# Graph network kernel on one core: the first two relation pairs projected node group by node group, and two passes over the nodes moved to GpSimd

## The reference, cut to what matters

```python
h = relu(layernorm(x)); agg = segment_sum(gate * core, dst)
x = x + layernorm(agg + h) * gamma + beta          # end of the first layer
h = relu(layernorm(x))                             # input of the second
proj = einsum('ni,rio->rno', h, Wf)                # 16 relations, 3125 nodes each
m = (proj[etype, src] + bias) / degree[dst]        # gathered by edge
x = x + 2 * (h @ loop_weight) + self_bias + segment_sum(m, dst) + backward pass
```

## Time and profile before

| What | us |
|---|---|
| median of three executions | 3847.81 |
| the lowest and the highest of them | 3843.88, 3848.78 |
| the profiled execution | 3849.95 |
| its span in the trace | 3848.1 |
| PE busy in the span | 3288.7 |
| DVE busy in the span | 2579.7 |
| POOL busy in the span | 2340.2 |
| ACT busy in the span | 976.2 |

### The profile page before, as it was taken

One profiled execution on the slowest core, in us unless ns is written; L12 is line 12 of the kernel. 1 busy time (PEld: TensorE's weight loads), 2 busy tenths in 40 slices (PEclk: granted clock), 3 DMA queues, 4 the chain that ended last, 5 costly groups with the idle time before them and its releaser, 6 DMA issues.

```text
span 3848.1 us, 74572 instructions
## 1 busy us (share of the span) xinstructions
PE 3288.7 (85%) x21136; PEld 2831.0 (74%) x21137; DVE 2579.7 (67%) x3930; ACT 976.2 (25%) x1654; POOL 2340.2 (61%) x2362
## 2 busy tenths in 40 slices
PE   6999999999999996998777778878857778787776
PEld 4999999999999995887665566666645666665654
DVE  6888888888888887887766673333354444444444
ACT  3555555555555544442000000000010000000000
POOL 1666655666665660002776677777777777777775
PEclk8999999999999998999989899999989999999999
DMA  5666666666565652664555557555533333333333
GB/s 173 174 171 171 172 171 168 171 168 169 167 169 164 170 160 84 208 209 160 158 163 153 151 154 164 166 157 161 160 97 105 104 102 98 100 105 104 104 105 114
DMA packets 322741, 569.88 MB, mean 148 GB/s; under 512 B 73895, under 2 KB 218389, under 8 KB 322581
## 3 DMA queue, kind: packets, MB, share of 16 engines
q0 software_dynamic: 137984, 411.19, 38.5%
q1 hardware_dynamic: 182732, 154.33, 12.2%
q10 hardware_dynamic: 1864, 2.52, 0.2%
HBM read 452.43 MB, written 115.41 MB: 148 GB/s over the span
## 4 chain that ended last, share of the span: by engine, by line
PE 64%; DVE 15%; issue 10%; POOL 4%; DMA 3%; DVEq 2%; ACT 1%; SPq 1%; ACTq 0%; POOLq 0%
PE pc L671 14%; PE pa L680 13%; PE pa L719 7%; PE pu L657 5%; DVE tops L1210 5%; PE pu L719 4%; PE pg L643 4%; DVE key L1213 4%; PE pg L719 4%; POOL fa L422 4%; PE pu L651 3%; PE pc L666 2%; DMA fa<-proj,gslot 2%; PE pu L775 2%; PE pg L775 1%
## 5 line engine op out<-in xcount | busy, mean ns | idle before, releaser
L422 POOL DMA_INDIRECT fa<-proj,gslot x1568 | 1503.5, 959 | 882.0 <-issue 436.8
L405 POOL DMA_INDIRECT fa<-ptab,slot x784 | 832.9, 1062 | 576.5 <-issue 298.9
L680 PE MATMUL pa<-fa,onehot 128*128 128x258 f32 x1760 | 471.0, 416 | 212.3 <-DVE onehot L994 141.4
L671 PEld LDWEIGHTS pc<-ws,hr 128*128 128x128 f32 x4704 | 607.1, 188 | 16.8
L671 PE MATMUL pc<-ws,hr 128*128 128x256 f32 x4704 | 614.0, 279 | 0.0
L994 DVE SCALAR_TENSOR_TENSOR fa<-pc,base,src_f 128x512 f32<-128x512 f32 x406 | 303.6, 751 | 450.0 <-PE pa L719 320.0
L680 PEld LDWEIGHTS pa<-fa,onehot 128*128 128x128 f32 x1760 | 349.6, 205 | 319.2 <-issue 264.0
L719 PE MATMUL pa<-fa 128*128 128x258 f32 x1568 | 373.5, 380 | 0.0
L719 PEld LDWEIGHTS pa<-fa 128*128 128x128 f32 x1568 | 297.0, 189 | 45.2
L719 PE MATMUL pu<-fa 128*128 128x258 f32 x784 | 198.9, 397 | 120.7 <-DVE acc L1051 82.5
L1000 DVE TENSOR_TENSOR fa<-fa,pc 128x1024 f32<-128x1024 f32 x196 | 239.4, 1221 | 92.4 <-PE pc L671 92.3
(11 more groups left out here) (151 smaller groups left out, 4934.9 us busy)
## 6 DMA issues: line engine op xcount, KB each, us to landing
proj<-fa SPq DMA_DIRECT2D x400, 256.0 KB, 2.3
fa<-in_ea_t SPq DMA_DIRECT2D x196, 128.0 KB
fa<-proj,gslot POOLq DMA_INDIRECT x1568, 2.8
fa<-ptab,slot POOLq DMA_INDIRECT x784
fa<-in_Wrel SPq DMA_DIRECT2D x32, 256.0 KB, 3.0
ptab<-fa SPq DMA_DIRECT2D x25, 256.0 KB, 2.0
out<-res SPq DMA_DIRECT2D x4, 768.0 KB
res<-in_x SPq DMA_DIRECT2D x1, 1792.0 KB, 20.4
```

The source lines that it names most:

```text
L405: pool.indirect_dma_start(pbuf[:, n % 2, j, :], None, ptab[:, :], bass.IndirectOffsetOnAxis(ap=slot[:, n, j:j + 1], axis=0)).then_inc(s_ga ...
L422: pool.indirect_dma_start(gbuf[:, n, j, 0:H], None, proj[k - 1][:, :], bass.IndirectOffsetOnAxis(ap=gslot[:, at, j:j + 1], axis=0)).then_i ...
L671: last = nc.tensor.matmul(pc[:, j, :], uT[:, par, a, j // 2, kk, j % 2 * P:(j % 2 + 1) * P], w2s[:, c, kk, :], start=False, stop=(j == jj ...
L680: last = nc.tensor.matmul(pa[:, bank, 0:width], keys[:, at, j, :], rows[:, j, :], start=(n == 0), stop=(n == len(todo) - 1))
```

## The change

Pairs 0 and 1 are both projected group by group. PE does the 5 blocks of a group for pair 0, three transposes of the next group, and then the 5 blocks for pair 1 with the other two transposes behind the first two of them. Within a slot the uses alternate between the pairs (`slot_use`, `projected`). ACT's `node_group` gets two loops: the first normalises the blocks of a group and copies out pair 1 of two groups before, alternating; the second copies out pair 0 and the transposed blocks. The low weights of pair 1 move up to DVE's third node group, and those of pair 2 from the head of the sort to behind its third step. The memset and the self bias addition move from DVE to GpSimd, behind the last transposed block; DVE waits for them just ahead of `add_own`. SP loads the weights of pairs 2 and 3 ahead of the first stores. The core of the diff:

```diff
+        def slot_use(q, b):
+            return 2 * (b // GB) + q if piped(q) else 5 * q + b // 5
+        def projected(q, b):
+            return 2 * GB * (b // GB) + GB * q + b % GB if piped(q) else NB * q + b
...
-            with sp.Fori(0, NQ // 4) as i:
+            for q in range(2):
+                sp.wait_ge(s_wlo, q + 1)
+                load_weights(q + 2, q)
+            for g in range(NB // GB):
+                for q in range(2):
+                    store_projections(q, 0, group(g))
+            with sp.Fori(1, NQ // 4) as i:
                 relations(i, 0)
...
+            pool.wait_ge(s_hT[1], NB)
+            nc.gpsimd.memset(acc[:, :, :], 0.0).then_inc(s_zero[0], 1)
+            nc.gpsimd.tensor_tensor(res[:, :, :], res[:, :, :], sbias_b[:, :].unsqueeze(1).to_broadcast([P, NB, H]),
+                                    ALU.add).then_inc(s_sb, 1)
             pool.wait_ge(s_zero[0], 1)
...
                 if past(q, 2):
-                    act.wait_ge(s_proj, NB * (q - 1))
+                    act.wait_ge(s_proj, 2 * NB - GB if isinstance(q, int) and q == 2 else NB * (q - 1))
...
                 if g == 0:
                     weights_high(0, 0, 0)
+                    weights_high(1, 1, 0)
+                for n in range(GB):
+                    if 1 <= g <= NB // GB:
                         normalise(2, group(g - 1)[n], res, ACT.Relu)
+                    if g >= 3:
+                        evacuate(act, nc.scalar.copy, 1, group(g - 3)[n])
+                for n in range(GB):
+                    if 2 <= g <= NB // GB + 1:
+                        evacuate(act, nc.scalar.copy, 0, group(g - 2)[n])
+                    if 1 <= g <= NB // GB:
+                        transposed_high(group(g - 1)[n])
...
             weights_high(2, 0, 1)
-            for b in range(NB):
-                evacuate(act, nc.scalar.copy, 1, b)
+            node_group(NB // GB + 2)
...
+            for b in group(0):
+                transposes(1, b)
             for g in range(NB // GB):
...
                 for b in group(g):
                     pe.wait_ge(s_hT[1], b + 1)
                     project(0, 0, b, 0)
+                later = group(g + 1) if g + 1 < NB // GB else []
+                for b in later[:3]:
+                    transposes(1, b)
+                if g == 0:
+                    pe.wait_ge(s_wlo, 2)
+                for n, b in enumerate(group(g)):
+                    project(1, 1, b, 0)
+                    for t in later[3 + n:4 + n]:
+                        transposes(1, t)
...
-                if g == 1:
-                    weights_low(0, 0)
+                if g in (1, 2):
+                    weights_low(g - 1, g - 1)
...
-            weights_low(1, 1)
...
-            nc.vector.memset(acc[:, :, :], 0.0).then_inc(s_zero[0], 1)
-            nc.vector.tensor_tensor(res[:, :, :], res[:, :, :], sbias_b[:, :].unsqueeze(1).to_broadcast([P, NB, H]),
-                                    ALU.add).then_inc(s_sb, 1)
...
+                    if also and n == 2:
+                        weights_low(2, 0)
...
-            weights_low(2, 0)
-            for q in range(2):
-                sort_relation(q)
+            sort_relation(0, also=True)
+            sort_relation(1)
...
+            dve.wait_ge(s_zero[0], 1)
+            dve.wait_ge(s_sb, 1)
             for b in range(NB):
                 add_own(b)
```

More of the change, by code:

```diff
@@ L251, in turned, with piped @@
             return bank.rearrange("p (k n) -> p k n", k=HK)
-        def evacuate(eng, copy, q, b):
[L255 to L260, removed]
+        def piped(q):
+            return isinstance(q, int) and q < 2
+        def slot_use(q, b):
+            return 2 * (b // GB) + q if piped(q) else 5 * q + b // 5
+        def projected(q, b):
+            return 2 * GB * (b // GB) + GB * q + b % GB if piped(q) else NB * q + b
+        def evacuate(eng, copy, q, b):
+            n, use = b % 5, slot_use(q, b)
+            eng.wait_ge(s_proj, projected(q, b) + 1)
+            if past(use, 1):
+                eng.wait_ge(s_pst[n], 16 * use)
             copy(pstage[n].rearrange("p r f -> p (r f)"), pslots[n]).then_inc(s_pev[n], 1)
@@ L324, in load_weights, with store_projections @@
                                  wv[bass.ds(q, 1), :, kk, :, :].rearrange("q p r f -> (q p) r f")).then_inc(s_wrel[par], 16)
-            def store_projections(q, d):
-                for b in range(NB):
+            def store_projections(q, d, blocks=range(NB)):
+                for b in blocks:
                     n = b % 5
-                    sp.wait_ge(s_pev[n], 5 * q + b // 5 + 1)
+                    sp.wait_ge(s_pev[n], slot_use(q, b) + 1)
                     sp.dma_start(pv[d][bass.ds(q - d * (NQ // 2), 1), :, b, :, :].rearrange("q p r f -> (q p) r f"),
@@ L549, in node_group @@
                     weights_high(0, 0, 0)
-                for n in range(GB + 1):
-                    if 1 <= g <= NB // GB and n < GB:
+                    weights_high(1, 1, 0)
+                for n in range(GB):
+                    if 1 <= g <= NB // GB:
                         normalise(2, group(g - 1)[n], res, ACT.Relu)
[L553 to L556, removed]
+                    if g >= 3:
[5 more added lines that the diff above has]
+                        transposed_high(group(g - 1)[n])
                 if g < NB // GB:
                     sqrt_var(2, g, GB * g, GB * (g + 1))
-                elif g == NB // GB:
-                    weights_high(1, 1, 0)
             for g in range(NB // GB + 2):
@@ L765, in project @@
             def project(q, u, b, d):
-                n = b % 5
-                if b >= 5 or past(q, 1):
-                    pe.wait_ge(s_pev[n], 5 * q + b // 5)
+                n, use = b % 5, slot_use(q, b)
+                if past(use, 1):
+                    pe.wait_ge(s_pev[n], use)
                 if d:
@@ L783, in forward_relations @@
                         project(2 * i + u, u, b, 0)
+            for b in group(0):
+                transposes(1, b)
             for g in range(NB // GB):
-                for b in group(g):
-                    transposes(1, b)
                 if g == 0:
@@ L792, in _ @@
                     project(0, 0, b, 0)
-            pe.wait_ge(s_wlo, 2)
-            for b in range(NB):
-                project(1, 1, b, 0)
+                later = group(g + 1) if g + 1 < NB // GB else []
[7 more added lines that the diff above has]
+                        transposes(1, t)
             with pe.Fori(1, NQ // 4) as i:
@@ L1219, in keep_sorted, with sort_relation @@
                 nc.vector.tensor_copy(srt[:, bass.ds(8 * it, 8 * n)], tops[:, 0:8 * n]).then_inc(s_sort, 1)
-            def sort_relation(q):
+            def sort_relation(q, also=False):
                 before = (2 * S1 + 1) * q
```

2 lines of the change are left out of this document (removed).

## The result

The changed kernel took 3856.74 us (median of 17 runs, 3850.31 to 3862.79), the kernel before 3844.61 in the same series (17 runs, 3840.15 to 3851.59). The ratio is 1.0030, with a 95% interval of 1.0022 to 1.0037: 12.1 us slower, 8.5 to 14.2. The forecast was 13.1 us slower, a median of 3860.9 in a range of 3849 to 3865. A second series, on another chip, gave 3856.57 beside 3847.01, ratio 1.0027 (1.0018 to 1.0037).

A forecast was written before the change was run, and what follows sets the result against it. The prediction took DVE's sort to end the stage, so its start and stops decide. Terms 2.9 + 0.4 + 1.7 + 8.1 = 13.1 us on 3847.81 gave 3860.9, range 3849 to 3865.

The forecast's parts named there:

- The rule: Whole stage: it ends when DVE's sort ends, 236 us after the sort starts; PE's gain does not count.
- the throttle of the last weight copy: End of the sort: the last weight copy ended only 2.1 us before DVE's subtraction that needs it.
- Steps 1 to 4: Node groups: PE stands 2.8 us ahead of groups 1 and 2; DVE's last transposed block comes 13.8 us later.
- Step 5: Behind three sort steps: DVE waits 4.1 us for pair 2's low weights; stage ends 2.9 us later.
- Step 6: Ahead of pair 3: PE idles about 12 us and may restart at its lower clock; 0 to 0.8, taken 0.4.
- Step 7: Node groups: PE's new gaps cause zero to two clock falls, 0 to 3.4 us; one taken, 1.7.
- Step 8: GpSimd: moved memset 4.9 us and addition 14.7 us, ending by 1559.3 to 1564.2, by itself free.
- Step 9: Pair 2's weight subtraction on DVE: held until GpSimd's addition ends; zero to 8.1 us, 8.1 taken.
- rival A: Pair 2's subtraction passes GpSimd's addition or is stretched only a microsecond: 5.0 us slower, 3852.8; chance 0.34.
- steps 1 to 7: Node groups to pair 3: sort delay 2.9, PE lag 0.4 and clock fall 1.7, together 5.0 us.
- rival B: Node groups: PE has no gaps because normalisations come earlier; 5.2 us less, 3842.6; chance 0.08.
- Rivals B and C: B: node groups without PE gaps, 3842.6, 0.08. C: sort starts 13.6 us earlier, 3834; with other gains 0.05.

## Why the prediction was right, point by point

**The rule (the sort ends the stage): shown.** With the throttle of the last weight copy it foretold that 13.6 us less DVE work gives 2 and not 13.6 (1.6 measured) and that load added is seen in full (13.7 added, 14.2 measured). That PE's 12 us ahead of pair 3 cost nothing is read from the changed kernel's own trace: from 1561.56 to the sort's end DVE never stood longer than 0.5 us and never for a weight copy, and `own` still had to wait 5.75 us for DVE.

**Steps 1 to 4: right, slightly short.** Gaps of 2.54 and 2.57 against 2.8, released by ACT's slot copy. Group 1 started at 1500.22 (1499.7 laid out), group 2 at 1519.30 (1517.1 and one fall), group 3 at 1536.92 (1532.8 and one fall). The last transposed block came 18.1 later in the first trace and 16.3 to 16.7 in the two others, against 13.8 + 1.7 = 15.5.

**Step 5: right.** A wait of 4.33 against 4.1.

**Step 6: right.** 12.10 us of idle PE ahead of pair 3, and the lower clock behind it (4.99 against 2.88). It cost nothing, where 0.4 was put on it: no later subtraction waited for its weights.

**Step 7: right in kind, short in size.** Groups 1 and 2 both started slow in the first trace; I had taken one fall for 1.7. In the two later traces only group 1 starts slow (4.58 and 4.48), and group 2 fast (2.97 in both), behind the same gap of 2.55. Of the nine traces with this order five have the last transposed block at 86.5 and four at 85.0. So the term was 1.7 or 3.4.

**Step 8: half right.** The memset took 5.50 (4.9 from the rows), the addition 14.33 (14.7). What failed is that the two follow one another: 6.92 us lie between.

**Step 9: wrong in this kernel.** Its 8.1 us were the largest term of the sum. The exclusion is real (11.30 and 9.10 us when the addition comes first) but the subtraction started first and took 1.23 us, so the term measured nothing. So what happened is rival A's path, 5.0 forecast and 6 to 8 found in the stretch, while the medians moved by 12.1. The forecast of 13.1 came close because a term that did not occur made up for clock falls of which I took too few and for up to 4 us that I can't place. The sign and the place rest on steps 1 to 7. That the loss would be above 0.2% rested on step 9 (0.46 of the 0.52), and this, like the closeness of the number, was luck. The step's other reason, that gathers of 1062 and 959 ns show GpSimd held by DVE, was not tested. In rival B, 45 blocks and 20 transposes from 1479.87 end at 1545.5 by the spacings given, not 1546.5; no chance hangs on that microsecond.

The Trainium skill, page "SBUF — State Buffer", section "Who interferes with whom", says that whichever of the two is second waits for the whole of the first. Three runs agree: the three held subtractions (11.30, 9.10 and 3.72 us) all ended 1.1 us after the addition. The page "GPSIMD Engine Reference" of the Trainium skill, section 2.1, speaks of about 6 us for the first call to a newly loaded kernel (there a routine of GpSimd's), with no instruction in the profile; the gaps here are 6.9 to 8.1 us, also marked only "issue". Set into my lay-out, an estimate from that figure would not have settled the order: the addition would have started at 1544.6 + 4.9 + 6 = 1555.5, just ahead of the subtraction at 1556.1. It would have shown that the term hung on less than a microsecond.

**Rivals B and C** did not occur; no trace has the node groups free of gaps or the transposes at their old times.

## What to carry to other kernels

Find the queue that ends the stage, then ask what holds that queue back if it gets lighter: here 13.6 us of work removed gave 2, and 13.7 us added cost all of itself in the stretch. When work moves to another engine, list which instructions it will meet there; two short passes that each read two SBUF operands can cost the length of the longer one, depending on which starts first. And a queue order that helps one engine (PE's second pair between the transposes) has to be paid for on the engine that ends the stage, unless that engine's idle time is filled as well.

## What the runs showed of the hardware

The first addition on GpSimd started 6.9 to 7.6 us after the memset ahead of it had ended, in six traces. After a small addition earlier it started at once. In the three kernels where it waited for `s_wlo` at that point anyway (9.10, 7.34 and 8.05 us) it started 0.1 us after the subtraction that released it had ended. So this time passes beside a semaphore wait. A max or replace of the sort inside a GpSimd addition ran at its usual length (0.96 to 0.98 us); a subtraction of two SBUF tiles that started inside one ended only 1.1 us after it. On two chips the kernel before took 4476 and 4548 us instead of 3847. The changed kernel's trace on the slower of them (4527.2 us beside 3855.5) has the stretch examined here at 328.4 us beside 328.5; 120 us of the difference lie ahead of it and 552 behind its end. Why is open.
